# A limit on scatters under way in the message stage of a graph network kernel: two semaphores in turn, each scatter begun when the last but one has landed

## The chip, the cores and the metric

The kernel runs on one core of one Trainium2 chip. The metric is the device time of one execution in microseconds (us). Three runs of the kernel before gave 6808.58, 6786.99 and 6791.19 us, a median of 6791.19 us. Besides these there is one profiled execution, from which all rows below come.

The engines go by these names: PE is TensorE, DVE is VectorE, ACT is ScalarE, POOL is GpSimd, SP is SyncE. A name with a q (POOLq, SPq) is the engine's sequencer, which handles waits, registers and DMA issues.

## What is computed

Two graph layers, each followed by a residual sum and a layer norm, over 6250 nodes with 160 features and 200000 edges. The changed part belongs to the first layer. For every edge the features of one end node and the edge's 32 attributes go through a bilinear product, and the result, a message of 160 numbers, is summed by node:

```python
s1 = jnp.einsum('ea,eb,abc->ec', xs, es, W1) * (1.0 / np.sqrt(MUL0_N * MUL0_E))
s2 = jnp.einsum('eai,ebi,abc->ec', xv, ev, W2) * (...)
v1 = jnp.einsum('ea,ebi,abc->eci', xs, ev, W3) * (...)
v2 = jnp.einsum('eai,eb,abc->eci', xv, es, W4) * (...)
...
messages = tp @ Wm + bm
agg = jax.ops.segment_sum(messages, row, num_segments=N_NODES)
```

The edges come sorted by `dst`, the sum goes by `src`. So the kernel writes each message to a place in a table in device memory that is ordered by source bucket, and a later stage reads that table bucket by bucket. The factor `Wm` is applied after the sum.

## The kernel before

The program has several stages, one after the other, separated by barriers. From about 150 to 2660 us of the span runs the message stage; then a stage that sums the messages by source node, to about 3400 us; then the second layer, to the end.

The message stage goes over the edges in 98 epochs (`EPOCHS`), each of 16 tiles (`EP`) of 128 edges. Loops run over pairs of epochs, t, with r = 0 or 1 for the two of a pair; n = t*2 + r is the epoch's number. Each engine has a program of its own, and the order is written out by hand with semaphores:

- SP loads the 1 MB of edge attributes of an epoch into `nat` with four DMAs (L982, `load_attributes`), as soon as DVE has read the last epoch's attributes.
- DVE (`masks`, L1103 to L1112; `products`, L1118; `select`, L1126) masks and transposes the attributes, and transposes the node products. In six of the seven spans it also works out places for the next span (`places`, L1057 to L1094).
- PE (`step_a` to `step_c`, L1298; `messages`, L1328) forms the node products and the messages. Two tiles' messages make one group g, of which an epoch has 8 (`PAIRS0`).
- ACT (`message`, L1237) copies each group from PSUM to `stage[:, r]`. Before the first group of an epoch it writes two small columns (L1243, L1246).
- POOL (`scatter`, L1015 to L1027) waits for each group's copy (`s_mev`), increments the counter `s_begun`, and issues two indirect DMAs, one per tile. Each scatters 128 rows of 162 floats (`MSG`), 83 KB, to the places in `place[:, r, k]`. Below, such a DMA is called a scatter.

`stage` and `place` have two halves, one per r. ACT may write half r again only when the 16 scatters of epoch n - 2 have landed. Each scatter adds 16 to a semaphore when it lands. Before the change the semaphore is `s_out[r]`, one per half, so ACT waits for t * (16 * EP) on it (L1242), and POOL waits for the same once per epoch (L1018). Within an epoch nothing holds a scatter back but the copy of its group and the engine itself. At the stage's end POOL waits until all have landed (L1035, L1036), and the stage's barrier follows.

Of the kernel before, what the change touches and what calls it, by code (L numbers as in the profile page):

```python
# [28 lines left out]
EP = 16  # L29
EPOCHS = TILES // EP  # L30
# [538 lines left out]
def gnn_kernel(nc, A, out, scratch):  # L569
# [14 lines left out]
    with outer:  # L584
# [15 lines left out]
        s_begun = sem_in(outer)("begun")  # L600
# [23 lines left out]
        with nc.cleanup_on_exit(), ExitStack() as ctx:  # L624
            sb, ps = sb_in(ctx), ps_in(ctx)

            def sem(n):
                return nc.alloc_semaphore(name=n)
# [11 lines left out]
            with ExitStack() as pro:  # L640
# [13 lines left out]
                first = sb("first", [P, BLOCKS])  # L654
# [258 lines left out]
            with ExitStack() as main:  # L913
# [17 lines left out]
                stage = sb("stage", [P, 2, EP, MSG])  # L931
# [11 lines left out]
                s_msg, s_mev, s_loc, s_place = sem("msg"), sem("mev"), sem("loc"), sem("place")  # L943
                s_out = [sem(f"out{r}") for r in range(2)]
                BANKS = len(ps_m)
# [23 lines left out]
                with nc.Block() as block:  # L969
# [41 lines left out]
                    def _(pool):  # L1011
# [3 lines left out]
                        def scatter(t, r, first=False):  # L1015
                            n = t * 2 + r
                            if not first:
                                pool.wait_ge(s_out[r], t * (16 * EP))  # L1018
                                pool.sem_inc(s_begun, 1)
                            pool.wait_ge(s_place, n + 1)  # L1020
                            pool.wait_ge(s_loc, n + 1)
                            for g in range(PAIRS0):
                                pool.wait_ge(s_mev, n * PAIRS0 + (BANKS + g + 1))
                                pool.sem_inc(s_begun, 1)
                                for k in (2 * g, 2 * g + 1):
                                    nc.gpsimd.indirect_dma_start(out=msgs, out_offset=bass.IndirectOffsetOnAxis(ap=place[:, r, k:k + 1], axis=0),  # L1026
                                                                 in_=stage[:, r, k, :], in_offset=None).then_inc(s_out[r], 16)  # L1027

# [3 lines left out]
                        with pool.Fori(1, EPOCHS // 2) as t:  # L1032
                            for r in range(2):
                                scatter(t, r)
                        for r in range(2):  # L1035
                            pool.wait_ge(s_out[r], 16 * EP * (EPOCHS // 2))  # L1036

# [167 lines left out]
                    def _(act):  # L1205
# [33 lines left out]
                        def epoch(t, r, counted, first=False, last=False):  # L1239
                            n = t * 2 + r  # L1240
                            if not first:
                                act.wait_ge(s_out[r], t * (16 * EP))  # L1242
                            nc.scalar.copy(stage[:, r, :, D0 + 1], loc[:, bass.ds(n * EP, EP)]).then_inc(s_loc, 1)  # L1243
# [2023 lines left out]
```

## Time and profile before

| | us |
|---|---|
| median of three runs | 6791.19 (6786.99 to 6808.58) |
| span of the profiled execution | 6574.9 |
| median less span (what lies around the span) | 216.3 |
| PE busy, whole span | 4404.1 (67%) |
| DVE busy, whole span | 4082.6 (62%) |
| POOL busy, whole span | 3046.1 (46%) |
| 1568 scatters (L1026) on POOL | 1506.8 busy, 961 ns each |
| mean granted TensorE clock | 0.753 of full speed |

The span is the time from the first to the last instruction of the profiled execution. Its own time as a run isn't recorded, so the median of the three runs stands beside it. The profile's busy time of a scatter on POOL is the time in which the engine worked on it; the data moves later, and shows in the rows of the DMA queues (q0 is POOL's, q1 is SP's). The share of the DMA is that of 16 engines.

### The profile page before, as it was taken

To read this page: it belongs to the slowest core of one execution; us is meant where nothing else is said; L and a number is where in the kernel's file an instruction comes from. 1 tells how busy PE (TensorE), PEld (TensorE's weight loads), DVE (VectorE), ACT (ScalarE), POOL (GpSimd) and SP (SyncE) were. 2 spreads that over 40 slices of the span, in tenths; PEclk is the share of its full clock that TensorE was granted. 3 is DMA by queue.
4 is the path that set the end of the run, shared out by engine and by line. 5 is a ranking of instruction groups with operands and counts; after the bars stand their busy time and mean duration, and the time that the engine had idled before them with its cause. 6 is when DMAs were issued, how large, how long until landed. Compare 5 with 4: busy or idle time off the path is not lost. (4 is left out here: it accounts for less than half of the span.)

```text
span 6574.9 us, 113593 instructions
## 1 busy us (share of the span) xinstructions
PE 4404.1 (67%) x32521; PEld 3293.8 (50%) x32521; DVE 4082.6 (62%) x7506; ACT 1176.2 (18%) x3413; POOL 3046.1 (46%) x3249
## 2 busy tenths in 40 slices
PE   3767777777776777799776655655655665565555
PEld 2545555555555555689564434444444444444444
DVE  7877778778787766577455445444544544544544
ACT  0322222222222222000120111111111111111111
POOL 0556666566665666100035444444444444444442
PEclk7877778888788777899886666676666667666666
DMA  3333333333333333688332222222222222222221
GB/s 133 94 94 100 94 101 97 98 95 99 94 101 93 101 94 103 216 271 274 119 97 54 48 49 49 48 49 49 49 50 49 48 47 51 48 49 48 50 47 32
DMA packets 602395, 572.30 MB, mean 87 GB/s; under 512 B 183060, under 2 KB 491412, under 8 KB 602308
## 3 DMA queue, kind: packets, MB, share of 16 engines
q0 software_dynamic: 150528, 258.71, 14.5%
q1 hardware_dynamic: 414772, 227.28, 13.7%
q10 hardware_dynamic: 37008, 85.28, 4.2%
q8 instruction: 38, 0.62, 0.0%
q14 instruction: 49, 0.40, 0.0%
HBM read 412.44 MB, written 158.52 MB: 87 GB/s over the span
## 5 line engine op out<-in xcount | busy, mean ns | idle before, releaser
L2299 POOL DMA_INDIRECT q_fg<-f,q_index x1568 | 1484.1, 946 | 1608.8 <-DVE q_prod L2353 1138.1
L1026 POOL DMA_INDIRECT messages<-stage,place x1568 | 1506.8, 961 | 993.3 <-ACT stage L1237 506.4
L2546 PE MATMUL q_ps_m<-q_prod,q_onehot_sh 128*32 128x160 f32 x12544 | 914.4, 426 | 1015.6 <-DVE q_sums L2367 850.2
L1328 PEld LDWEIGHTS ps_m<-by_attr,turned 128*128 128x128 f32 x6272 | 1096.5, 226 | 281.3 <-issue 246.8
L2367 DVE SCALAR_TENSOR_TENSOR q_sums<-q_ps_m,split_q,q_sums 128x161 f32 x784 | 301.2, 384 | 1485.4 <-remote 1294.9
L1328 PE MATMUL ps_m<-by_attr,turned 128*128 128x160 f32 x6272 | 1204.7, 353 | 17.6 <-issue 13.0
L2546 PEld LDWEIGHTS q_ps_m<-q_prod,q_onehot_sh 128*32 128x32 f32 x12544 | 541.7, 150 | 1330.3 <-DVE q_sums L2367 908.4
L1298 PE MATMUL ps_y<-w_xy,xt 32*128 32x256 f32 (+3 forms) x1176 | 476.9, 705 | 488.0 <-ACT xz L1209 250.8
L2533 PE MATMUL q_ps_w<-q_wfc,q_hidden 64*128 64x192 f32 x3136 | 514.6, 425 | 206.6 <-DVE q_prod L2353 145.3
L1237 ACT COPY stage<-ps_m 128x320 f32<-128x320 f32 x784 | 337.2, 435 | 1737.9 <-PE ps_m L1328 848.1
L1118 DVE STREAM_TRANSPOSE by_attr<-by_node 128x2048 f32<-128x2048 f32 (+1 forms) x294 | 548.0, 1915 | 2.7 <-ACT by_node L1212 2.7
L1490 PE MATMUL ps_g<-rows_in,local 128*128 128x161 f32 x3328 | 464.7, 301 | 76.3 <-DVE local L1450 76.3
L2533 PEld LDWEIGHTS q_ps_w<-q_wfc,q_hidden 64*128 64x128 f32 x3136 | 367.0, 245 | 266.5 <-DVE q_prod L2353 165.2
L1490 PEld LDWEIGHTS ps_g<-rows_in,local 128*128 128x128 f32 x3328 | 458.4, 190 | 83.6 <-DVE local L1450 83.6
L2447 ACT ACTIVATE q_hidden<-q_ps_h 128x256 f32<-128x256 f32 x392 | 129.1, 381 | 1940.6 <-remote 1871.3
L1298 PEld LDWEIGHTS ps_y<-w_xy,xt 32*128 32x128 f32 (+1 forms) x1176 | 148.7, 234 | 648.2 <-ACT xz L1209 266.0
L1109 DVE SCALAR_TENSOR_TENSOR masked<-ps_at,quarter,nat 128x2048 f32<-128x2048 f32 x196 | 460.8, 2351 | 7.0
L1112 DVE STREAM_TRANSPOSE turned<-masked 128x2048 f32<-128x2048 f32 x196 | 453.1, 2312 | 6.7
L2353 DVE TENSOR_TENSOR q_prod<-q_ps_w,q_fg 128x384 f32<-128x384 f32 x784 | 395.7, 545 | 0.0
L1212 ACT ACTIVATE by_node<-ps_y 128x256 f32<-128x256 f32 (+1 forms) x980 | 388.5, 485 | 17.7 <-PE ps_y L1298 17.7
L1103 DVE CAST ps_at<-rel_t 128x64 f32 (+1 forms) x98 | 22.3, 228 | 453.5 <-PE ps_m L1328 368.4
L1298 PE MATMUL ps_y<-w_z,xz 32*128 32x512 f32 (+1 forms) x392 | 217.9, 641 | 128.0 <-ACT by_node L1212 112.0
(247 smaller groups left out, 4487.3 us busy)
## 6 DMA issues: line engine op xcount, KB each, us to landing
nat<-in_edge_attr SPq DMA_DIRECT2D x392, 256.0 KB
rows_in<-messages ACTq DMA_DIRECT2D x208, 324.0 KB, 3.4
rows_in<-messages SPq DMA_DIRECT2D x208, 324.0 KB, 3.4
messages<-stage,place POOLq DMA_INDIRECT x1568
q_fg<-f,q_index POOLq DMA_INDIRECT x1568
messages<-zeros ACTq DMA_DIRECT2D x49, 324.0 KB, 2.2
q_a<-in_edge_attr SPq DMA_DIRECT2D x196, 64.0 KB
xw<-in_x SPq DMA_DIRECT2D x98, 80.0 KB
```

The costliest lines, as they stand in the source:

```text
L1026: nc.gpsimd.indirect_dma_start(out=msgs, out_offset=bass.IndirectOffsetOnAxis(ap=place[:, r, k:k + 1], axis=0), in_=stage[:, r, k, :], in_ ...
L1109: nc.vector.scalar_tensor_tensor(masked[:, :, :], at, quarter[:, half:half + 1], nat[:, :, :].rearrange("p t (j w) -> p (t j) w", w=32), A ...
L1112: nc.vector.transpose(turned[:, r, half, :], masked[:, :, :].rearrange("p t w -> p (t w)")).then_inc(s_turn, 1)
L1118: nc.vector.transpose(by_attr[:, r, :, c, :].rearrange("p k c h -> p c k h"), by_node[:, r, c, :]).then_inc(s_attr, 1)
L1212: nc.scalar.activation(by_node[:, r, c, b], bank[:, at:at + size].rearrange("p (b c) -> p c b", b=8), ACT.Copy, scale=factor).then_inc(s_e ...
L1298: return nc.tensor.matmul(bank[:, at:at + cols.stop - cols.start], source[rows, :], weights[rows, cols], start=True, stop=True, tile_posit ...
L1328: last = nc.tensor.matmul(ps_m[g % BANKS][:, k % 2 * D0:k % 2 * D0 + D0], turned[:, r, half, k * P:(k + 1) * P], by_attr[:, r, k, :, half] ...
L1490: last = nc.tensor.matmul(ps_g[u % BANKSZ][:, 0:W1_], local[:, u % RINGZ, j, :], rows_in[:, u % RINGZ, j, 0:W1_], start=(j == 0), stop=(j ...
L2299: nc.gpsimd.indirect_dma_start(out=fg[:, i, place_of(v), :], out_offset=None, in_=f_tab, in_offset=bass.IndirectOffsetOnAxis(ap=index[:, i ...
L2353: last = nc.vector.tensor_tensor(prod[:, h % 2, at, part, NS:D0].rearrange("p v (i u) -> p v i u", u=NV), w[:, :, c:c + NV].unsqueeze(2).b ...
L2533: last = nc.tensor.matmul(ps_w[:, g, half, b, 0:192], hidden[rows, par, 2 * g + b, :], wfc2[rows, :], start=True, stop=True, tile_position ...
L2546: nc.tensor.matmul(ps_m[strip, 0:D0], oh_sh[:, strip], prod[:, h % 2, g * QUAD + place_of(v), 1 if c < 3 else 0, :], start=(v == 0), stop= ...
```

## The change

The two semaphores are no longer one per half but take turns by tile: scatter k of an epoch signals `s_out[k % 2]`. Before scatter k POOL waits until the scatter before the last on the same semaphore has landed, so that at most two are under way. The counter `s_begun` is incremented once per scatter and not once per group. The wait at the start of an epoch on POOL is dropped, and ACT's wait before it writes a half, as well as POOL's at the end, is for both semaphores.

```diff
-                s_out = [sem(f"out{r}") for r in range(2)]
+                INFLIGHT = 2
+                s_out = [sem(f"out{r}") for r in range(INFLIGHT)]
+                LANDS = 16 * (EP // INFLIGHT)
...
                         def scatter(t, r, first=False):
                             n = t * 2 + r
-                            if not first:
-                                pool.wait_ge(s_out[r], t * (16 * EP))
-                                pool.sem_inc(s_begun, 1)
                             pool.wait_ge(s_place, n + 1)
                             pool.wait_ge(s_loc, n + 1)
                             for g in range(PAIRS0):
                                 pool.wait_ge(s_mev, n * PAIRS0 + (BANKS + g + 1))
-                                pool.sem_inc(s_begun, 1)
                                 for k in (2 * g, 2 * g + 1):
+                                    landed = n * LANDS + k // INFLIGHT * 16
+                                    if not isinstance(landed, int) or landed > 0:
+                                        pool.wait_ge(s_out[k % INFLIGHT], landed)
+                                    pool.sem_inc(s_begun, 1)
                                     nc.gpsimd.indirect_dma_start(out=msgs, out_offset=bass.IndirectOffsetOnAxis(ap=place[:, r, k:k + 1], axis=0),
-                                                                 in_=stage[:, r, k, :], in_offset=None).then_inc(s_out[r], 16)
+                                                                 in_=stage[:, r, k, :], in_offset=None).then_inc(s_out[k % INFLIGHT], 16)
...
-                        for r in range(2):
-                            pool.wait_ge(s_out[r], 16 * EP * (EPOCHS // 2))
+                        for landed in s_out:
+                            pool.wait_ge(landed, LANDS * EPOCHS)
...
                             if not first:
-                                act.wait_ge(s_out[r], t * (16 * EP))
+                                for landed in s_out:
+                                    act.wait_ge(landed, (n - 1) * LANDS)
```

## Rows read from the trace of the kernel before

**Rows 1.** Busy time by stage: PE, PEld, DVE, ACT, POOL, then clock, DMA share, GB/s
```profile
150.00:2657.00 2507.00, 1847.04 (x8266) 1333.65 (x8266) 1922.22 (x2137) 723.83 (x2163) 1513.66 (x1570) 0.79 0.37 97
...
3400.00:6574.00 3174.00, 1864.13 (x18884) 1327.40 (x18883) 1548.59 (x3854) 384.93 (x1037) 1484.75 (x1570) 0.67 0.21 49
```

**Rows 2.** First CAST of DVE's masks in each epoch: count, durations, first and last start
```profile
L1103 DVE CAST ps_at<-rel_t x98: 222/228/229, 158.2 to 2606.8; 128x64 f32 x96, 128x64 f32<-128x64 uint8 x2
```

**Rows 3.** Who waited for whom from 400 to 2590 us: total, times, longest
```profile
ACT stage L1237 <- PE ps_m L1328: 757.0, 249, 7.7
...
DVE ps_at L1103 <- PE ps_m L1328: 344.6, 68, 13.4
...
POOL messages L1026 <- ACT stage L1237: 458.1, 237, 3.9
POOL messages L1026 <- issue: 401.2, 1151, 2.7
...
SPq L982 <- DVE masked L1109: 1189.1, 63, 26.9
```

**Rows 4.** Scatters and ACT's copies, whole stage: durations in ns, first and last start
```profile
L1026 POOL DMA_INDIRECT messages<-stage,place x1568: 954/960/1890, 190.1 to 2656.4; - x196
...
L1237 ACT COPY stage<-ps_m x784: 410/427/492, 188.6 to 2632.8; 128x320 f32<-128x320 f32 x196
```

**Rows 5.** Timeline of ACT: start, duration, what
```profile
1008.33 0.43 ACT L1237 COPY stage<-ps_m 128x320 f32<-128x320 f32 x1 [6.78 <-remote]
...
1014.69 0.43 ACT L1237 COPY stage<-ps_m 128x320 f32<-128x320 f32 x1 [4.56 <-PE ps_m L1328]
```

**Rows 6.** Timeline of POOL in the same stretch
```profile
1009.57 0.96 POOL L1026 DMA_INDIRECT messages<-stage,place  x1 [3.47 <-ACT stage L1237]
1010.83 0.96 POOL L1026 DMA_INDIRECT messages<-stage,place  x1 [0.30 <-issue]
...
1015.93 0.96 POOL L1026 DMA_INDIRECT messages<-stage,place  x1 [1.60 <-ACT stage L1237]
```

**Rows 7.** POOL's sequencer passing the wait for a copy (L1023) and increment
```profile
L1024 POOLq EVENT_SEMAPHORE  x1: 17/17/17, 1008.8 to 1008.8; - x1
```

**Rows 8.** POOL's sequencer passing the stage's last wait for landings
```profile
L1036 POOLq EVENT_SEMAPHORE  x1: 17/17/17, 2658.7 to 2658.7; - x1
```

**Rows 9.** Timeline at the end of the stage, all engines
```profile
2655.14 0.96 POOL L1026 DMA_INDIRECT messages<-stage,place  x1 [0.30 <-issue]
2656.41 0.96 POOL L1026 DMA_INDIRECT messages<-stage,place  x1 [0.30 <-issue]
...
2661.59 0.62 DVE L1175 TENSOR_SCALAR split_q<-ps_at,row_no 128x392 f32<-128x392 f32 x1
2669.33 6.94 POOL L1441 MEMSET acc<- 128x8211 f32 x1 [11.96 <-POOLq L624]
```

**Rows 10.** Short windows behind the last scatter, columns as in Rows 1
```profile
2656.40:2657.10 0.70, 0.00 (x0) 0.00 (x0) 0.00 (x0) 0.00 (x0) 0.69 (x1) 0.50 0.39 119
2657.10:2657.90 0.80, 0.00 (x0) 0.00 (x0) 0.00 (x0) 0.00 (x0) 0.27 (x1) 0.50 0.00 0
2657.90:2658.40 0.50, 0.00 (x0) 0.00 (x0) 0.00 (x0) 0.00 (x0) 0.00 (x0) 0.50 0.46 166
2658.40:2660.30 1.90, 0.00 (x0) 0.00 (x0) 0.00 (x0) 0.00 (x0) 0.00 (x0) 0.50 0.00 0
```

**Rows 11.** Timeline of SP's queue and POOL around one load of attributes
```profile
1023.52 0.96 POOL L1026 DMA_INDIRECT messages<-stage,place  x1 [0.30 <-issue]
1023.76 4.20 SPq L982 DMA_DIRECT2D nat<-in_edge_attr  x4
1024.79 0.96 POOL L1026 DMA_INDIRECT messages<-stage,place  x1 [0.30 <-issue]
```

**Rows 12.** DMA queues in 1024.4 to 1027.0 us: packets, MB, share of 16 engines
```profile
q1 hardware_dynamic: 951, 0.48, 67.5%
q0 software_dynamic: 48, 0.08, 9.7%
```

**Rows 13.** The same in 1027.0 to 1029.4 us
```profile
q1 hardware_dynamic: 974, 0.48, 105.1%
q0 software_dynamic: 37, 0.08, 15.2%
```

**Rows 14.** The same in 1029.4 to 1029.8 us
```profile
q0 software_dynamic: 25, 0.06, 62.5%
q1 hardware_dynamic: 110, 0.05, 49.0%
```

**Rows 15.** DMA queues over the whole span: packets, MB, share of 16 engines
```profile
q0 software_dynamic: 150528, 258.71, 14.5%
```

**Rows 16.** Register work of POOL's sequencer for its waits, 400 to 2590 us
```profile
L1023 POOLq ALU_OP  x607: 32/32/32, 401.9 to 2589.2; - x152
```

**Rows 17.** ACT's first write of an epoch and its register work, 400 to 2590 us
```profile
L1243 ACTq FUSED_REGOPS  x87: 60/60/60, 409.3 to 2584.3; - x87
```

## The prediction

> **What bounds the kernel now.** I read the busy times by stage first. The change touches the message stage alone, some 2500 of 6575 us, and there no engine is full: of 2507 us PE is busy 1847, DVE 1922, ACT 724, POOL 1514 [rows 1]. So the stage is bound by a chain between engines. The pace of that chain comes from a row of DVE that stands once in each epoch: 98 starts from 158.2 to 2606.8 us, which is 2448.6 / 97 = 25.2 us per epoch [rows 2]. The waits say who sets it: ACT waits for PE's messages (757 us of 2190), DVE waits for them too (345 us), and POOL waits for ACT's copies (458 us), while SP waits for DVE before it may load attributes (1189 us) [rows 3]. POOL stands at the end of this chain. It takes what ACT gives, and its only way back is the half of `stage` that ACT may write again once the scatters of epoch n - 2 have landed. No wait of ACT on that shows in the view of waits. So POOL has slack now, and the question is how much.
>
> The slack: first scatter at 190.1, last at 2656.4 us, and POOL passes the final wait at 2658.7 [rows 4, 8]. That is 2468.6 us for 1568 scatters, 1.574 us each, or 25.2 us for the 16 of an epoch. Inside a burst, where scatters stand queued, one follows the other after 0.96 + 0.30 = 1.26 us [rows 6], 20.2 us for 16. POOL thus has 5.0 us of slack per epoch. The change is free as long as a scatter costs no more than 1.574 us on average.
>
> **What the change costs, part by part.**
>
> *The limit itself.* Scatter k can start only when k - 2 has landed. So the time of a pair of scatters becomes: start of one to the moment at which POOL's sequencer sees it landed, and from there to the start of the next but one. Both pieces are in the trace.
>
> First piece, the flight. The last scatter starts at 2656.41 and the sequencer passes the wait for its landing at 2658.7, 2.3 us later [rows 8, 9]. The windows behind it show where that goes: no DMA traffic from 2657.1 to 2657.9, traffic until 2658.4, none after [rows 10]. So the data is gone at about 1.9 us, and 0.4 us go by until the semaphore is seen. 1.9 is the lower bound of the flight, 2.3 what a waiting sequencer sees; I take 2.3, since the new wait is of that very kind.
>
> Second piece, the restart. A sequencer that has run dry shows it: ACT's copies end at 1008.76 and 1015.12, and POOL's next scatters start at 1009.57 and 1015.93, both 0.81 us later [rows 5, 6]. The sequencer's increment behind the wait is at 1008.8, so 0.8 us lie between passing the wait and the scatter's start [rows 6, 7]. Now this is hidden: in a burst the sequencer has handed over the next scatter while the engine is at the last one, and only 0.30 us show [rows 6]. With a wait ahead of every scatter it is hidden no longer. The bounds are 0.30 (it overlaps after all) and 0.81; I take 0.8, since the new wait stands directly ahead of the scatter, as the wait for the copy does in these rows.
>
> Sum: 2.3 + 0.8 = 3.1 us for two, 1.55 us each, 24.8 us for 16. That is still under the 25.2 us of the chain. Were this all, the change would cost nothing.
>
> *The loads of attributes.* Once in each epoch SP loads 1 MB, and the flight is longer while it runs. One epoch shows by how much. The four issues begin at 1023.76 [rows 11]. A scatter has 48 packets (150528 / 3136 scatters and gathers) [rows 15]. The scatter started at 1023.52 would have moved its data by 1025.4; POOL's queue moves just 48 packets up to 1027.0, so it is up to 1.6 us late [rows 11, 12]. The next one, started at 1024.79, was due at 1026.7; its 96th packet (48 + 37 by 1029.4, 25 more by 1029.8) passes between 1029.4 and 1029.8, 2.7 to 3.1 us late [rows 11 to 14]. SP's queue has 68 to 105% of the engines in this time. With at most two under way, one scatter of each of the two alternating chains is caught by each load, and a delay of the one and of the other moves their common pace by the mean, (1.6 + 2.9) / 2 = 2.2 us. Not every load catches them in the worst phase, so I take 2.0 us per epoch. The bounds are 0 (a load falls where POOL waits for a copy) and 3.1.
>
> Epoch of POOL: 24.8 + 2.0 = 26.8 us. This is 1.6 us more than the chain's 25.2, so POOL becomes the bound. ACT then waits at the start of each epoch for the landings of epoch n - 2, and behind ACT stand PE (PSUM banks not copied) and DVE (its `turned` halves not free). Two halves of `stage` decouple the two paces, so that an epoch of PE and ACT that takes longer than the mean is covered by the backlog on POOL, and the sum goes by POOL's pace alone.
>
> Sum for the stage: 98 x 26.8 = 2626 us against 2468.6, +158 us.
>
> *The stage's end.* POOL passes its last wait at 2658.7, DVE ends at 2662.2, and POOL begins the next stage at 2669.33 [rows 8, 9]. A POOL that is 158 us later is the last by far; at most 3.5 us of the shift are covered by DVE. I leave this out.
>
> *Small parts.* POOL's sequencer has a wait and an increment more for every second scatter and a register operation of 32 ns [rows 16], in the time in which it waits for a landing anyway: 0. If it were uncovered it would be 16 x 0.05 = 0.8 us per epoch. ACT's additional wait is one more register operation of 60 ns per epoch [rows 17]; it stands behind a wait that ends later: 0, or 98 x 0.06 = 6 us. The dropped wait of POOL at an epoch's start was met long before: 0.
>
> *PE's clock.* A longer epoch lowers PE's busy share from 74% to some 69%. The granted clock is 0.79 here and 0.67 in the last stage, where PE is busy 59% [rows 1]. If it falls to 0.75, PE's 18.6 us per epoch grow by about 1 us, and the chain needs 26.2, still under 26.8.
>
> *What the Trainium skill says.* The flight of 2.3 us can be set beside the Trainium skill's page "DMA: Bandwidth & Descriptors", section "Anatomy of one DMA — SWDGE (gpsimd) path", which gives 2.0 us plus the bytes over 436 GB/s, here an estimate of 2.19 us for 83 KB; the trace agrees within 0.1 us. Taken alone it speaks against my sum: two under way at 2.19 us each give one per 1.10 us, faster than the 1.26 us of a burst, and the limit would never be felt. The same section also says that a wait is made on the issuing sequencer before dispatch, which is what leaves the restart uncovered.
>
> **The rivals.**
>
> *The limit is hidden (not slower).* The pace of PE, ACT and DVE goes on setting the epoch. It happens if the mean per scatter stays under 1.574 us. With a restart of 0.30 us the pair is 2.6 us and the epoch 20.8 + 2.0 = 22.8 us; with a flight of 1.9 us it is 21.6 + 2.0 = 23.6 us. With my two values and a load term under 0.4 us it is just met too. For it speaks that already now only 2.3 / 1.26 = 1.8 scatters are under way outside the loads, so the number alone changes little. Against it speaks that both restarts and the one final wait are read directly from rows. It gives 6791 us, plus up to 8 us if a backlog is worked off at the slower pace at the stage's end (between ACT's last copy at 2632.8 and the last scatter some 23.6 / 1.26 = 19 scatters are worked off; 19 x 0.3 = 6) [rows 4].
>
> *The loads cost more.* If a load keeps both chains back for the 3.1 us of the second scatter and the restart is 0.81 us, the epoch is 24.9 + 3.1 = 28.0 us and the sum 98 x 28.0 - 2468.6 = +275 us: 7066 us.
>
> *Faster.* Fewer scatters queue up during a load, so that the load itself ends sooner. The load isn't on the chain: SP waits 1189 us for DVE, and DVE's waits name PE and not the load [rows 3]. A load would have to hold DVE back for this to give anything. Nothing here ties the chain's stalls to a load; at 0.5 us per epoch, an eighth of the 4 us that DVE waits for PE per epoch (345 us over 87 epochs), it gives 6742 us.
>
> **How the numbers follow.** POOL's pace at 26.8 us per epoch: 6791.2 + 158 = 6949 us, with its own range of 6850 (load term 1.0) to 7066, chance 0.70. The costlier loads beyond 7066: 0.09. Hidden: 0.17. Faster: 0.04. The span of the profiled execution should be 6574.9 + 158 = 6733 us; some 216 us lie around it and stay. The range reaches from the hidden case to the costlier load, 6790 to 7066. A measurement of this kernel can tell about 0.3%, 20 us, from no change, 0.2 us per epoch. Slower by more: 0.79. Within: 0.17. Faster: 0.04.
>
> **What would show it.** Step by step in the profile after: scatters in a burst start in a rhythm that takes 3.1 us for two, not 2.5; during a load a gap of 4 to 6 us for two; POOL's waits are no longer put down to ACT's copy but to its own landings (they may be named issue or remote); ACT has idle time ahead of L1243 or L1246, some 1.6 us per epoch; DVE's row L1103 comes every 26.8 us; the last scatter starts near 2814 us; stages behind have the same lengths. I would be wrong if pairs come at 2.6 us (the restart overlaps), if they come at 3.1 us but the epochs at 25.2 (the loads cost less than the slack), or if ACT waits for nothing new.

## The result and the profile after

The changed kernel takes 7080.59 us (median of 4 runs, 7059.09 to 7091.82) against 6789.09 us before (6786.42 to 6808.58): ratio 1.0426, 95% interval 1.0397 to 1.0454. It is slower by 291 us. The forecast was +158 us, with a range that ended at 7066 us. The sign and the mechanism were right; the sizes were not, that of the load term above all. The profiled execution took 7091.82 us with a span of 7090.2.

The three main stretches of the changed kernel; columns as in [rows 1]:

```profile
150.00:3003.00 2853.00, 1826.55 (x8266) 1284.40 (x8266) 1922.31 (x2139) 712.50 (x2164) 1512.77 (x1570) 0.76 0.33 85
3003.00:3750.00 747.00, 644.93 (x4287) 592.49 (x4288) 497.84 (x1223) 54.12 (x192) 41.09 (x103) 0.95 0.67 207
3750.00:7090.00 3340.00, 1826.52 (x18866) 1305.82 (x18866) 1542.64 (x3847) 382.29 (x1034) 1483.16 (x1568) 0.66 0.19 46
```

Read the first row against the first of [rows 1]. Each engine is busy for the same time as before, within 21 us, but the stretch is 346 us longer. So nobody does more work. Somebody waits.

The scatters, the first CAST of DVE in each epoch, and the last wait for landings; count, durations in ns, first and last start:

```profile
L1028 POOL DMA_INDIRECT messages<-stage,place x1568: 954/958/1655, 190.1 to 3001.9; - x196
L1105 DVE CAST ps_at<-rel_t x98: 221/228/229, 158.2 to 2913.4; 128x64 f32 x96, 128x64 f32<-128x64 uint8 x2
...
L1038 POOLq EVENT_SEMAPHORE  x1: 17/17/17, 3004.2 to 3004.2; - x1
```

From 190.1 to 3001.9 us are 2811.8 us for 1568 scatters: 1.79 us each, 28.7 us per epoch. The forecast had 26.8. DVE's row comes every 28.4 us ((2913.4 - 158.2) / 97). The last scatter is seen landed 2.3 us after its start, as in [rows 8, 9]; the flight itself didn't change.

Who waits, from 400 to 2590 us, to be read against [rows 3] (total us, times, longest):

```profile
ACT stage L1246 <- DMA messages<-stage,place: 806.6, 76, 14.5
ACT stage L1239 <- PE ps_m L1331: 700.6, 195, 6.3
...
POOL messages L1028 <- issue: 467.7, 794, 7.1
...
POOL messages L1028 <- DMA messages<-stage,place: 442.4, 325, 4.4
...
POOL messages L1028 <- ACT stage L1239: 110.2, 103, 4.6
```

POOL waited 458.1 us for ACT's copies before; now it is 110.2, and its own landings stand in their place. ACT has a wait that [rows 3] doesn't have: 76 times, so once in each epoch of this stretch, it stands ahead of the epoch's first write for the landings of epoch n - 2. The roles are exchanged: POOL sets the pace, and ACT, PE and DVE follow it.

POOL in steady rhythm and around one load (start, duration, what, idle before it and its releaser), with SP's issues and ACT's restart among it:

```profile
1016.42 0.96 POOL L1028 DMA_INDIRECT messages<-stage,place  x1 [0.92 <-issue]
...
1019.57 0.96 POOL L1028 DMA_INDIRECT messages<-stage,place  x1 [0.93 <-DMA messages<-stage,place]
...
1022.70 0.96 POOL L1028 DMA_INDIRECT messages<-stage,place  x1 [0.90 <-DMA messages<-stage,place]
1024.11 0.96 POOL L1028 DMA_INDIRECT messages<-stage,place  x1 [0.46 <-issue]
1027.77 0.96 POOL L1028 DMA_INDIRECT messages<-stage,place  x1 [2.70 <-ACT stage L1239]
1030.33 0.96 POOL L1028 DMA_INDIRECT messages<-stage,place  x1 [1.59 <-DMA messages<-stage,place]
1031.59 0.96 POOL L1028 DMA_INDIRECT messages<-stage,place  x1 [0.30 <-issue]
1033.52 0.96 POOL L1028 DMA_INDIRECT messages<-stage,place  x1 [0.97 <-issue]
```

```profile
1022.48 1.91 SPq L984 DMA_DIRECT2D nat<-in_edge_attr  x4
```

```profile
1027.14 0.22 ACT L1246 CAST stage<-loc 128x16 f32 x1 [11.65 <-DMA messages<-stage,place]
```

Every second start is 3.15 us after the last but one (1016.42, 1019.57), against 2 x 1.26 in [rows 6]. That is the 3.1 us of the forecast. Then SP issues its four transfers at 1022.48, and the pairs grow. Follow the two alternating chains. One goes 1022.70, 1027.77, 1031.59: 5.07 and then 3.82 us, where 3.13 is the rule, so it is late by 1.9 and once more by 0.7, together 2.6 us. The other goes 1024.11, 1030.33, 1033.52: 6.22 and 3.19, late by 3.1 us. This load thus costs (2.6 + 3.1) / 2 = 2.9 us. The gap ahead of 1027.77 is put down to ACT. But ACT itself begins only at 1027.14, released by a landing too, and writes the other half of `stage`; what came late is the landing of the scatter of 1022.70.

That is one load. I counted the others of this profile in the same way: the lateness of both chains over four pairs, against a rhythm of 3.13 us, for the 81 loads that no stall (last section) falls on; late means by over 0.25 us. The mean cost is 3.3 us per load, the least 2.3. In 54 of them one chain is late twice, as here; in 17 each chain is late just once. Both kinds cost the same, 3.2 and 3.3 us in the mean. Of the two chains the one that is less late is late by 3.1 us in the mean, the other by 3.4.

**An unusual profile of before.** The forecast took from the profile that 216 us lie around the span (6574.9 against a time of 6791). But in the profile of after, span and time differ by 1.6 us (7090.2 and 7091.82), and in a second profile of the kernel before, on a faster chip, by 1.7 (5051.4 and 5053.12). So nothing lies around the span; the profiled execution of before was itself some 3% quicker than the runs beside it. Why isn't known; its granted clock was 0.753, and that of the runs of this kernel at 6777 to 6821 us was 0.737 to 0.743. The experiment with eight under way ran at the speed of before (ratio 0.9987) with a span of 6789.6; its scatters and its last stage's gathers are a better yardstick than [rows 4]:

```profile
L1028 POOL DMA_INDIRECT messages<-stage,place x1568: 954/960/1893, 189.8 to 2697.1; - x196
...
L2302 POOL DMA_INDIRECT q_fg<-f,q_index x1568: 940/946/1324, 3456.6 to 6707.0; - x196
```

The message stage takes 2507 us there, 25.6 per epoch (2466 in [rows 4]), and the gathers 3250 us. The changed kernel's gathers, 3763.4 to 7008.7 us, take 3245. So the stages behind kept their length, and the message stage grew by 2812 - 2507, some 305 us.

### The profile page after: what moved, and what is told of

It is laid out like the page before. It is cut to its first block and busy times, and to the rows that moved or that the text cites. A ratio compares the mean times of both kernels' runs of the same rounds, so it can differ in the third digit from the quotient of the medians.

```text
span 7090.2 us, 115144 instructions
## 1 busy us (share of the span) xinstructions
PE 4349.9 (61%) x32521; PEld 3225.4 (45%) x32521; DVE 4078.0 (58%) x7506; ACT 1163.2 (16%) x3413; POOL 3044.0 (43%) x3249
## 5 line engine op out<-in xcount | busy, mean ns | idle before, releaser
L2549 PE MATMUL q_ps_m<-q_prod,q_onehot_sh 128*32 128x160 f32 x12544 | 881.9, 428 | 1143.3 <-DVE q_sums L2370 1000.6
L1331 PEld LDWEIGHTS ps_m<-by_attr,turned 128*128 128x128 f32 x6272 | 1049.7, 217 | 290.9 <-issue 205.0
L1331 PE MATMUL ps_m<-by_attr,turned 128*128 128x160 f32 x6272 | 1151.2, 342 | 24.0 <-ACT stage L1239 24.0
L1301 PE MATMUL ps_y<-w_xy,xt 32*128 32x256 f32 (+3 forms) x1176 | 537.0, 784 | 916.9 <-ACT xz L1211 699.4
L1453 DVE TENSOR_TENSOR local<-iota,rows_in 128x512 f32<-128x512 f32 x416 | 280.8, 685 | 65.5 <-POOL acc L1444 54.3
```

Source lines behind the costliest of these rows:

```text
L1301: return nc.tensor.matmul(bank[:, at:at + cols.stop - cols.start], source[rows, :], weights[rows, cols], start=True, stop=True, tile_posit ...
L1331: last = nc.tensor.matmul(ps_m[g % BANKS][:, k % 2 * D0:k % 2 * D0 + D0], turned[:, r, half, k * P:(k + 1) * P], by_attr[:, r, k, :, half] ...
L2549: nc.tensor.matmul(ps_m[strip, 0:D0], oh_sh[:, strip], prod[:, h % 2, g * QUAD + place_of(v), 1 if c < 3 else 0, :], start=(v == 0), stop= ...
```

## The experiments

The chips were not alike. On some of them the kernel before took about 6790 us, on others 5058 us. So ratios are given only against the kernel before on the same chip; across chips the length of the message stage (first to last scatter) is compared, and the run of the changed kernel on a faster chip, told with the cut load, shows why it may be.

**The kernel before, again.** No edit.

> The kernel before, for a second profile. The profile read for the prediction had a span of 6574.9 us beside runs of 6789 us, and that of the kernel after a span of 7090.2 beside its own time of 7091.8. If the first profile was an unusually quick execution, this one has a span about 2 us below its time of some 6789 us, with the last stage (the second layer) some 150 us or more longer than 3158 us, and the message stage then tells how much of the change's cost lies in it. If instead some 216 us do lie around the span, its span is near 6575 us again.

5053.12 us, on one of the faster chips (13 other runs there: 5059.65, 5056.32 to 5063.84). The expected 6789 us were those of the other chips, but the span lies 1.7 us under the time, as it should when nothing lies around it. The message stage takes 2089 us, 21.3 per epoch:

```profile
L1026 POOL DMA_INDIRECT messages<-stage,place x1568: 954/960/1772, 190.1 to 2279.4; - x196
```

**The change again, and the same with eight and with four under way.** `INFLIGHT = 2` (as it is), `8` and `4`:

```diff
-                INFLIGHT = 2
+                INFLIGHT = 8
```

> The kernel after, unchanged, beside the kernel before on this run's chip. The profile of e1 showed that chips differ: there the kernel before took 5053 us, its message stage 2089 us (first to last scatter), where the first chip needed 6789 and 2466. Theory (POOL's own pace, made of semaphores and DMA, bounds the stage, so that it doesn't depend on the chip's granted TensorE clock): the stage takes 98 x 28.7 = 2812 us again, to 30 us, on any chip; where the kernel before takes 5060 us, this takes about 5060 + 2812 - 2089 = 5783 us. Rival (the cost is added to the chain of PE, ACT and DVE): the difference to before stays near 290 us, 5350 us.

> INFLIGHT = 8 in the kernel after. Four under way cost 43 us (0.8%) on the chip where POOL's slack is 21.3 - 20.2 = 1.1 us per epoch. Theory (these 43 us are landings during a load: 6.3 us of flight, receipt and restart over four is 1.6 us each, above 1.27): with eight the limit can never be felt (0.8 us each) and the time is that of before, within 10 us. Rival (each wait, increment and register operation on POOL or ACT costs by itself): it stays 40 us above before.

> INFLIGHT = 4 in the kernel after: same waits, increments and register work on POOL, four scatters may be under way. Theory (the pace is flight plus restart over the number under way): 3.1 / 4 = 0.8 us per scatter is under the 1.26 us of a burst, and the longest flight during a load, 5.2 + 0.4 + 0.8 = 6.4 us, gives 1.6 us each, within the slack: 6789 us, within 20 us. Rival (the added waits and increments cost by themselves, or the waits on two semaphores by ACT): it stays near 7080 us, above 6900 at least.

Two again: 7064.11 us, ratio 1.0386 (1.0361 to 1.0411), stage 2807 us. Eight: 6791.70 us, ratio 0.9987 (0.9970 to 1.0005), stage 2507 us. Four: ratio 1.0079 (1.0062 to 1.0095) on a chip of 5060 us, stage 2142 us against 2089 there. So the change's cost is the limit alone. With eight under way the waits and increments that stand ahead of every scatter cost nothing that can be measured, and even four under way costs 43 us where the chain is faster, twice the 20 us that were allowed for no change. The stage of two again lies within the expected 30 us of 2812.

```profile
L1028 POOL DMA_INDIRECT messages<-stage,place x1568: 954/958/1730, 189.6 to 2996.4; - x196
```

```profile
L1028 POOL DMA_INDIRECT messages<-stage,place x1568: 954/961/1470, 190.1 to 2331.6; - x196
```

(Two, then four under way.)

**The restart.** The pair was forecast as flight plus a restart that nothing hides. Five increments instead of one stand behind the wait, and, as the control, four more ahead of each scatter in the kernel before:

```diff
-                                    pool.sem_inc(s_begun, 1)
+                                    for _ in range(5):
+                                        pool.sem_inc(s_begun, 1)
```

> The kernel after with five increments of the counter instead of one between the wait for the landing and the scatter. Theory (what POOL's sequencer does behind the wait is uncovered, once for each pair of scatters): with about 0.07 us per increment the pair grows from 3.1 by 4 x 0.07 = 0.28 us, an epoch by 2.2 us, the kernel by some 220 us against e5. Rival (the sequencer overlaps with the engine as it did before): no difference to e5.

> The kernel before with four additional increments of the counter ahead of each scatter, the control of e7. Theory (in the kernel before, what the sequencer does stands behind the engine's work of 1.27 us per scatter): no change, within 0.3% of before. Rival (additional increments cost in either kernel, some 4 x 0.08 x 1568 = 490 us of sequencer time that the slack of 5 us per epoch would have to absorb in part): slower by more than 20 us.

Changed kernel: 7299.99 us, ratio 1.0737 (1.0718 to 1.0755), 236 us more than two again on the same chip, where 220 were expected. Kernel before: ratio 1.0001 (0.9992 to 1.0011). The stage with longer restarts:

```profile
L1029 POOL DMA_INDIRECT messages<-stage,place x1568: 954/958/1698, 190.0 to 3218.7; - x196
```

It grew by 3028.7 - 2806.8 = 222 us, or 0.28 us for each of 784 pairs, 0.07 us per increment. The same increments are free in the kernel before. What stands between a landing and the next scatter is thus on the path in the changed kernel and hidden in the kernel before, as the forecast said.

**One under way.** `INFLIGHT = 1`, with whole and with small loads (1/16 of the attributes is loaded, and the rest of the messages is formed from stale ones):

```diff
-                INFLIGHT = 2
+                INFLIGHT = 1
```

> INFLIGHT = 1 in the kernel after: each scatter begins when the last has landed. Theory (pace = flight plus restart over the number under way, plus what a load adds): 3.13 us per scatter, 50.1 us per epoch, 0.4 for a stall once in 112 scatters, and 3 to 4 us for the load, which now always meets one scatter and part of a second: 53.5 to 54.5 us per epoch, a message stage of 5240 to 5340 us from first to last scatter, whatever the chip. Rival (the restart is partly hidden with one under way, because POOL's sequencer has nothing else to do): under 50 us per epoch, 4900 us.

> INFLIGHT = 1 with the attribute loads behind the first epoch cut to one tile of 16 (messages from stale attributes). Theory: 50.1 + 0.4 + 0.3 = 50.8 us per epoch, a stage of 4980 us; the difference to e9 is the load term alone, 3 to 4 us per epoch (290 to 390 us). Rival (loads matter only through two scatters queueing behind each other): the difference to e9 is under 1 us per epoch.

Ratios 1.6223 (1.6190 to 1.6255) and 1.5715 (1.5683 to 1.5746). The rhythm with whole loads, and both stages:

```profile
1011.47 0.96 POOL L1028 DMA_INDIRECT messages<-stage,place  x1 [2.17 <-DMA messages<-stage,place]
1014.59 0.96 POOL L1028 DMA_INDIRECT messages<-stage,place  x1 [2.17 <-DMA messages<-stage,place]
```

```profile
L1028 POOL DMA_INDIRECT messages<-stage,place x1568: 959/962/2222, 189.8 to 5427.7; - x196
```

```profile
L1029 POOL DMA_INDIRECT messages<-stage,place x1568: 959/962/2084, 189.7 to 5170.1; - x196
```

A scatter alone takes 3.12 us from start to start: the same 2.3 + 0.8. One under way gives one scatter in this time, two give two. The stage with whole loads ends 2 us under the expected 5240 to 5340, that with small ones at the expected 4980. Whole loads cost 5238 - 4980 = 257 us here, 2.6 us per epoch, and not the expected 3 to 4. Counted over the profile, 87 of 95 loads delay just one scatter.

**The loads, made smaller.** Less of each load behind the first is fetched, 1/16, 1/2 or 3/4 of the attributes; the rest of each epoch's messages is formed from stale attributes. The kernel before with 1/16 is the control. The edit for 1/2:

```diff
-                                sp.dma_start(nat[32 * q:32 * q + 32, :, :], attr[:, bass.ds(n * EP, EP), :]).then_inc(s_nat, 16)
+                                size = EP if isinstance(n, int) and n == 0 else EP // 2
+                                sp.dma_start(nat[32 * q:32 * q + 32, 0:size, :], attr[:, bass.ds(n * EP, size), :]).then_inc(s_nat, 16)
```

> The kernel after, with the attribute loads behind the first epoch cut to one tile of 16 (64 KB in place of 1 MB per epoch; the messages are then formed from stale attributes). Theory (POOL's pace is 3.1 us per pair plus a term of the loads, 3.7 us per epoch): the load term goes, POOL's epoch is 25.0 us, as long as the chain's 25.2: 6790 to 6840 us, pairs at 3.1 us throughout. Rival (the loads have nothing to do with it and the excess comes from the coupling of the two paces): it stays above 6950 us.

> The kernel before with the same cut of the attribute loads, as the control. Theory (the loads aren't on the chain of PE, ACT and DVE, and POOL has slack): no change, 6789 us within 20 us. Rival (DVE or PE waits for the loads): faster, 6700 us or less, and then the gain of the run above must be read against this one.

> The kernel after with the attribute loads behind the first epoch cut to half (8 of 16 tiles, 0.5 MB; the other half of each epoch's messages is formed from stale attributes). Theory (a load keeps back both scatters under way, in proportion to its length): the message stage lies between e3's 2527 us (1/16 of a load) and e5's 2812 us, near 2670 us. Rival (a load costs a fixed amount each time it meets two scatters): near 2812 us.

> The kernel after with the attribute loads behind the first epoch cut to 12 of 16 tiles (0.75 MB; the rest of each epoch's messages from stale attributes). So far the stage took 2527 us with 1/16 of a load, 2584 with half, 2807 with all. Theory (a load costs what it lasts beyond the flight that a scatter has anyway, so the cost starts at about half a load and then grows in proportion): near 2695 us. Rival (it costs in proportion from zero, and the run with half a load was an exception): near 2745 us.

Ratios: 1.0866 (1.0847 to 1.0884) for 1/16 and 1.1123 (1.1101 to 1.1146) for 3/4, both on chips of 5060 us; 1.0066 (1.0040 to 1.0091) for 1/2 on a chip of 6797 us. The control: 1.0003 (0.9993 to 1.0012), so the kernel before doesn't feel its loads at all. The stages, for 1/16, 1/2 and 3/4:

```profile
L1029 POOL DMA_INDIRECT messages<-stage,place x1568: 955/959/1672, 190.1 to 2717.2; - x196
```

```profile
L1029 POOL DMA_INDIRECT messages<-stage,place x1568: 954/958/1534, 190.1 to 2774.0; - x196
```

```profile
L1029 POOL DMA_INDIRECT messages<-stage,place x1568: 954/958/1879, 190.0 to 2846.9; - x196
```

2527, 2584 and 2657 us, and 2807 to 2812 with the whole. Two things follow. First, with hardly a load left the epoch is 25.8 us and not 24.8. Second, the step from 1/16 to half the load costs 57 us, the next quarter 73 and the last quarter 150. No expectation had this: the 2670 us expected for half and the 2695 for three quarters were both too long, and the forecast's 2.0 us per epoch (196 us) stands against 280 to 285 us. The cost isn't in proportion to the bytes. (The run with half loads was on a slower chip, those with 1/16 and 3/4 on faster ones.)

**The load cut in two, and the pace on a faster chip.** SP waits between the second and the third transfer; the kernel before with the same cut is the control:

```diff
                             for q in range(4):
+                                if q == 2 and not (isinstance(n, int) and n < 2):
+                                    sp.wait_ge(s_attr, n * 3)
```

> The changed kernel (two scatters under way), each epoch's attribute load of four 256 KB transfers cut in two halves: SyncE issues the third and fourth only once the first two have landed. The same bytes are loaded, nothing is left out. Theory (the length of one uninterrupted stretch of load traffic sets the cost, and more than in proportion): two half loads cost about twice what one half load cost (26.4 - 25.8 = 0.6 us per epoch), so the message stage is 2527 + 2 x 57, about 2640 us, against 2807 to 2812 with the whole load. Rival (the bytes set it, however they are cut): the stage stays at 2800 to 2820 us. Between them, if the second half still meets scatters that the first half has delayed: 2660 to 2780.

> The changed kernel itself, again, beside the other two on one chip. Theory (the pace of the message stage is set by landings and by GpSimd, not by TensorE's clock, so it doesn't depend on the chip): the stage takes 2800 to 2815 us, 28.6 us per epoch, also on a chip where the kernel before runs in 5058 us; the whole then takes about 5058 + 2809 - 2089 = 5778 us there, ratio 1.142. On a chip where the kernel before runs in 6790 us: 7060 to 7080. Rival (the stage scales with the chip, as the kernel before does, 2089 against 2507 us): ratio 1.04 on either chip.

> Control: the kernel before with the attribute loads cut in two halves in the same way, nothing left out. Theory: its scatters are not held up by one another's landing, and a load that lands some 6 us later is still an epoch early, so the time is that of the kernel before within 0.3%. Rival (the later load holds up the epoch that needs it): slower by over 0.3%, and then the gain of the split in the changed kernel is understated by as much.

The expectation calls this a wait for the landing of the first two transfers. It isn't: `s_attr` is incremented by DVE's three transposes of the node products, so the third and fourth transfer wait until DVE has done those of the epoch before. In the profile the second half follows some 7.7 us behind the first, right at the end of these transposes:

```profile
1033.59 8.59 SPq L986 DMA_DIRECT2D nat<-in_edge_attr  x4
```

```profile
1035.66 5.59 DVE L1122 STREAM_TRANSPOSE by_attr<-by_node 128x2048 f32<-128x2048 f32 x3
```

```profile
1041.28 0.89 SPq L986 DMA_DIRECT2D nat<-in_edge_attr  x2
```

(The first line spans all four issues, the third shows the last two alone.) So the two halves are further apart than intended, which makes the test of an uninterrupted load no weaker.

Cut in two: 5804.36 us, ratio 1.1451 (1.1430 to 1.1473). Not cut: 5781.00 us, ratio 1.1415 (1.1396 to 1.1434). Control: 1.0010 (1.0000 to 1.0020). The stages, cut and not cut:

```profile
L1030 POOL DMA_INDIRECT messages<-stage,place x1568: 954/958/1888, 189.8 to 3035.5; - x196
```

```profile
L1028 POOL DMA_INDIRECT messages<-stage,place x1568: 957/962/1496, 189.9 to 3000.9; - x196
```

The length of an uninterrupted load was the wrong idea: 2846 us cut, 2811 not cut, and 2640 were expected. But the expectation for the changed kernel was met within 3 us: on this chip it took 5781.00 us, 5778 were expected. The stage takes 2811 us whatever the chip, because landings and POOL set its pace, while the kernel before needs 2507 us on one chip and 2089 on the other. The same change costs 4% there and 14% here.

**The load at another place in the epoch.** The loads fell on the scatters around the epoch's boundary. SP now waits in addition until scatter k = 2 of POOL's epoch has landed:

```diff
+                        def epoch_in(t, r, late):
...
+                            sp.wait_ge(s_mask, t * 4 + 2 * r)
+                            if late:
+                                sp.wait_ge(s_out[0], (t * 2 + r - 3) * LANDS + 32)
+                            load_attributes(t, r)
```

(`late` is true from t = 2 on.)

> The changed kernel (two scatters under way), whole attribute loads, nothing left out, but each load waits in addition until scatter k = 2 of GpSimd's present epoch has landed, so that it meets scatters in the middle of the steady rhythm and not the four around the epoch's boundary (k = 15, 0, 1, 2). Theory (the bytes set the cost, wherever they meet the scatters): the stage stays at 2790 to 2850 us. Rival (the boundary makes it dear: there GpSimd also waits for a copy and ScalarE restarts): load term back at about 2.0 us per epoch, stage 25.8 + 1.5 = 27.3 us per epoch, 2675 us. Second rival (the later load holds up VectorE): the stage is longer than 2850 us and waits for the attributes show.

> The changed kernel itself once more beside the other, for the ratio of the two on one chip: stage 2800 to 2815 us, as in the other profiles of it.

```profile
L1034 POOL DMA_INDIRECT messages<-stage,place x1568: 954/962/2043, 189.6 to 2997.8; - x196
```

```profile
1032.68 0.96 POOL L1034 DMA_INDIRECT messages<-stage,place  x1 [0.39 <-issue]
1038.09 0.96 POOL L1034 DMA_INDIRECT messages<-stage,place  x1 [4.44 <-DMA messages<-stage,place]
1039.35 0.96 POOL L1034 DMA_INDIRECT messages<-stage,place  x1 [0.31 <-issue]
```

Ratios 1.0404 (1.0371 to 1.0437) and 1.0391 (1.0360 to 1.0422), stages 2808 and 2798 us (the second 2 us under the expected 2800). At this other place the load costs the same. SP issued at 1030.69 here, and the delay shows as one gap of 4.44 us in the midst of the rhythm: both chains are late once, by 3.6 us (1031.33 to 1038.09) and by 3.5 us (1032.68 to 1039.35).

**The load offered more slowly.** Half a load was cheap, and two half loads one after the other were not. One thing in which they differ: a half load came as four transfers of 128 KB, the halves of the cut load as two of 256 KB each. SP issues one about each 0.5 us. So the whole attributes were loaded as eight transfers of 128 KB:

```diff
-                                sp.dma_start(nat[32 * q:32 * q + 32, :, :], attr[:, bass.ds(n * EP, EP), :]).then_inc(s_nat, 16)
+                                for c in range(0, EP, EP // 2):
+                                    sp.dma_start(nat[32 * q:32 * q + 32, c:c + EP // 2, :], attr[:, bass.ds(n * EP + c, EP // 2), :]).then_inc(s_nat, 16)
```

(DVE's wait for the attributes counts the eight transfers.)

> The changed kernel (two scatters under way) with the whole attributes, nothing left out, but each load comes as eight transfers of 128 KB instead of four of 256 KB. SyncE issues one about each 0.5 us, so the load is offered at 128 KB per 0.5 us, as the half loads were, and no longer at 256 KB per 0.5 us, and takes about as long as before (4 to 6 us). Theory (the backlog sets the cost: offered faster than the engines move it, the load queues up in front of the scatters; the half loads never built one up): the load term is twice that of the half loads, 2 x 57 us over 2527, so the message stage is about 2640 us, up to 2700. Rival (the bytes alone set it): 2800 to 2850 us, as with the whole, the split and the later loads.

```profile
L1029 POOL DMA_INDIRECT messages<-stage,place x1568: 954/958/2132, 189.7 to 2868.6; - x196
```

```profile
1012.28 3.85 SPq L985 DMA_DIRECT2D nat<-in_edge_attr  x8
```

5646.82 us, ratio 1.1161 (1.1142 to 1.1179), stage 2679 us, 132 us less than with four transfers, for the same bytes and within the expected 2640 to 2700 (the 5781 us were on another chip, of the same speed: 5058.92 us before here). What the DMA engines did: busy share in tenths, one digit per 0.6 us, from 1008 to 1032 us, of the kernel with half loads, with the cut load, with eight transfers, and of the changed kernel:

```profile
DMA  0040396985310040300403003112003040030400
```

```profile
DMA  2000003699951000303100304003030040300300
```

```profile
DMA  0040210318998999971004030040300202200304
```

```profile
DMA  2012003030040300303002102189999999640002
```

Half a load in small transfers brings the engines to a 9 in two slices with a 6 between them; half a load in large ones in three in a row; the whole load in large ones in seven in a row; the whole load in small ones in six, with an 8 among them. Small transfers are offered at 128 KB per 0.5 us, some 260 GB/s, large ones at 520. Together with the scatters' 83 KB per 1.57 us (53 GB/s) even the small ones are more than the changed kernel's engines moved in full slices (203 to 311 GB/s by the row of GB/s under the digits). The cost over 2527 us fell from 284 to 152 us and not to the 114 of two half loads.

Shown is that the same bytes in eight smaller transfers, issued over 3.85 us and not 1.91, cost about half. Not shown is why. The reading that the load queues up ahead of the scatters when it is offered faster than the engines move it fits the half loads, but with the whole load the engines stand at 8 or 9 for eight slices either way. Nor do the runs separate the rate of the issues from the size of a single transfer. Why the cost grows by 57, 73 and 150 us with the bytes stays open too.

## Why the prediction was right and wrong, step by step

- *The pair, 2.3 + 0.8 = 3.1 us.* Right. 3.15 us in the changed kernel's rhythm, 3.12 us for one scatter alone, and 0.28 us more when four increments were added to the restart. The rival with a hidden restart (2.6 us) is out. The Trainium skill's page "DMA: Bandwidth & Descriptors", section "Anatomy of one DMA — SWDGE (gpsimd) path", has a wait made on the issuing sequencer before dispatch; the trace agrees: one scatter alone comes every 3.12 us, and not every 2.3.
- *24.8 us per epoch without loads.* 1.0 us short: 2527 us are 25.8 us per epoch with 1/16 of the loads. Of this, 8 pairs of 3.13 instead of 3.1 us are 0.2 us. Some 0.4 us is a stall of both chains once in 112 scatters (below). The rest, 0.4 us, is left to the small loads and the node loads of 80 KB, which stand beside each load of attributes and were not costed; no run took them away.
- *The load term, 2.0 us per epoch.* This is the step that failed. By the stages it measured 280 to 285 us over the kernel with 1/16 of the loads (270 with the shortest of the changed kernel's four profiles), 2.9 us per epoch; it stood under the forecast's upper bound of 3.1. The forecast read two late scatters from [rows 12 to 14] (1.6 and 2.9 us), took their mean, 2.2, and shaved it to 2.0 for loads that fall badly. There are no such loads: each of the 81 counted ones costs at least 2.3 us, and the stage was as long (2808 us) when they were moved. And the first scatter's 1.6 us was too small a lateness for a chain: in the changed kernel both chains are held back by nearly the same, 3.1 and 3.4 us in the mean against the rhythm of 3.13. Their mean, 3.3, lies above the 2.9 of the stages by about what the kernel with 1/16 loses per load by the same count, 0.3 us. That a chain can be late twice in one load isn't what made the term larger, since the loads that caught each chain once cost as much.
- *The baseline, 25.2 us.* Wrong by 0.4. [rows 2] came from a quick execution; 25.6 us is the pace of the kernel with eight under way, which runs at the median's speed. This error hid a part of the others: with 26.8 against 25.6 the sum would have been +119 us.
- *The sum.* 28.7 = 24.8 + 1.0 + 2.9, against 25.6: 3.1 us x 98 = 304 us, by the stages 305. The spans of these two profiled executions differ by 300.6 us (7090.2 and 6789.6). The medians moved by 291, 267 and 268 us in three comparisons; single executions of one kernel lie 20 to 45 us apart in them (7059 to 7092 us for the changed kernel), and the last stage takes 3235 to 3250 us in these profiles.
- *"216 us lie around the span".* Wrong, as told above. Here a span 3% under the time of the same kernel meant that the profiled execution wasn't typical, and not that something lies around it.
- *ACT's idle time, 1.6 us per epoch.* 806.6 / 76 = 10.6 us. The forecast took the difference of the two paces. But ACT's whole idle time ahead of its copies and first writes grew by 3.7 us only, from 17.9 to 21.6 us per epoch (87 and 76 epochs in the stretch). The wait for PE stayed (8.7 and 9.2 us); the new wait stands in place of these two of before:

```profile
ACT stage L1237 <- remote: 530.2, 103, 16.8
...
ACT stage L1237 <- issue: 267.5, 99, 8.7
```

  After, no wait on remote is left and 131.4 us on issue. The size of a new wait isn't the size of its cost.
- *PE's clock.* 0.76 was measured, 0.75 forecast, and it costs nothing, since PE isn't on the path: on the faster chip the granted clock fell from 0.89 to 0.76 in this stage and the stage is as long as on the slower one.
- *Small parts at nothing.* Right: eight under way has them all and stands at 0.9987.
- *The rivals.* "The loads cost more" has a load keep both chains back for 3.1 us, which is what the count shows (3.1 and 3.4), and its epoch of 28.0 was the nearest; measured were 28.7. Nothing of the hidden limit or of a gain was found.

## What to carry to other kernels

In these runs a limit on transfers under way cost nothing where flight plus restart, divided by the limit, stayed well under the pace of the rest (eight under way); and the flight must be taken with the traffic that runs beside it, not from the quiet end of a stage (four under way cost 43 us on a faster chip). When transfers are gated by landings, a delay of one is passed on to its whole chain, and another queue's bursts, harmless before, become the term that decides: cost them at their upper reading for every chain, or try them as more and smaller transfers. Look at the span beside the run's time first: if the two don't agree, take the paces of before from a second profile. And look up who increments the semaphore that an experiment waits on.

## What the runs showed of the hardware

- **The pace of the chip.** The same kernel before took 5058 us on some chips and 6790 on others. Its message stage and its last stage on the faster, and the same stretches on the slower one (eight under way); columns as in [rows 1]:

```profile
150.00:2282.00 2132.00, 1673.78 (x8266) 1234.20 (x8266) 1922.71 (x2139) 716.31 (x2164) 1514.51 (x1570) 0.89 0.43 114
3040.00:5050.00 2010.00, 1401.95 (x18816) 1071.96 (x18816) 1545.06 (x3821) 385.54 (x1021) 1484.78 (x1565) 0.83 0.32 76
```

```profile
150.00:2700.00 2550.00, 1838.53 (x8260) 1326.84 (x8260) 1922.54 (x2137) 717.05 (x2159) 1513.74 (x1570) 0.79 0.36 95
3457.00:6707.00 3250.00, 1772.53 (x18383) 1264.95 (x18383) 1498.24 (x3721) 366.47 (x991) 1480.97 (x1568) 0.66 0.20 47
```

DVE, ACT and POOL are busy for the same time; PE isn't (1674 against 1839 us), and its granted clock is 0.89 against 0.79, and 0.83 against 0.66. But 165 us of PE don't make 418 us of the stage. What else differs wasn't settled.

- **A stall once in 112 scatters.** In the kernel with two under way and small loads, far from any load, both chains stand still at once:

```profile
1451.81 0.96 POOL L1029 DMA_INDIRECT messages<-stage,place  x1 [0.84 <-DMA messages<-stage,place]
1455.85 0.96 POOL L1029 DMA_INDIRECT messages<-stage,place  x1 [3.08 <-issue]
1457.12 0.96 POOL L1029 DMA_INDIRECT messages<-stage,place  x1 [0.30 <-issue]
...
1635.47 0.96 POOL L1029 DMA_INDIRECT messages<-stage,place  x1 [2.89 <-issue]
```

The late starts are 179.6 us apart, and 112 scatters lie between them. All through this profile it is each 112th scatter that lands late: 13 times in 1568, by some 2.8 us, 0.4 us per epoch. In the changed kernel the same positions fall together with a load, since 112 scatters are just seven epochs, and the chains are late by up to 6.6 us:

```profile
1402.16 0.96 POOL L1028 DMA_INDIRECT messages<-stage,place  x1 [7.08 <-issue]
```

With one under way and small loads the stalls come once in 113 scatters (starts at 548.60 and 908.03 us), so they aren't tied to the epochs of 16. In the kernel before nothing waits for such a landing. Their cause wasn't settled.
